# Attention on one NeuronCore: where TensorE's values product stands beside the transpose of the row maxima

## The reference

```
# "lat", layer 1: 16 heads of 16, rotary halves, causal
q, k, v = up(down(x))                  # latent projections
out = softmax(q k^T / 4 + causal mask) v
# "duo", layer 3: 16 heads of 16, two sets of keys, not causal
scores   = q k^T  / 4 ;  out_std = softmax(scores)   v
scores_p = q k'^T / 4 ;  out_p   = softmax(scores_p) v
out = (alpha * out_std + (1 - alpha) * out_p) W_O^T
```

## Time and profile before

| what | value |
|---|---|
| median of the runs | 3963.47 us (3 runs, 3954.07 to 3995.41) |
| span of the profiled execution | 3973.2 us |
| TensorE matmul busy | 3374.1 us, 85% of the span |
| VectorE busy | 2548.2 us, 64% |
| ScalarE busy | 2045.4 us, 51% |
| mean granted TensorE clock | 0.935 |
| lat units | about 545 to 843 us of the span |
| duo units | about 3190 to 3750 us of the span |

### The profile page before, as it was taken

How to read it: one execution, slowest core, us unless ns; L and a number is a source line. 1 busy time by engine, 2 the same in 40 slices (tenths; PEclk the granted TensorE clock), 3 DMA queues, 4 the chain that set the end, 5 groups by cost and what they waited for, 6 DMA issues and landing times. The chain is left out here.

```text
span 3973.2 us, 61781 instructions
## 1 busy us (share of the span) xinstructions
PE 3374.1 (85%) x20332; PEld 2517.7 (63%) x20332; DVE 2548.2 (64%) x3841; ACT 2045.4 (51%) x4432; POOL 1894.6 (48%) x1640
## 2 busy tenths in 40 slices
PE   1969989989986888888888888988887889999868
PEld 0659866668974666666666666666665655555544
DVE  6341155643126999999999999999997444444441
ACT  0332223332227777787777777877764344444422
POOL 0023200000316889888898889888885000000035
PEclk9879999999997999999999999999999989989965
DMA  3059710002951111111111111111110000000035
GB/s 97 2 185 334 268 63 1 1 18 106 331 207 34 44 33 44 33 44 36 42 45 44 37 42 34 43 42 35 33 43 22 26 1 1 1 1 1 3 109 174
DMA packets 133931, 264.41 MB, mean 67 GB/s; under 512 B 13888, under 2 KB 104504, under 8 KB 123096
## 3 DMA queue, kind: packets, MB, share of 16 engines
q1 hardware_dynamic: 122264, 229.24, 17.5%
q0 software_dynamic: 11328, 30.95, 2.3%
HBM read 233.64 MB, written 26.51 MB: 65 GB/s over the span
## 5 line engine op out<-in xcount | busy, mean ns | idle before, releaser
L1481 POOL TENSOR_TENSOR ssm_hc<-ssm_hs,ssm_cb 128x1024 f32<-128x1024 f32 x512 | 1204.5, 2356 | 179.0 <-PE ssm_py L1595 158.4
L1981 DVE TENSOR_TENSOR_SCAN ssm_hs<-ssm_da,ssm_pb 128x512 f32<-128x512 f32 x1024 | 1222.6, 1208 | 94.3 <-POOL ssm_hc L1481 89.5
L1595 PE MATMUL ssm_py<-ssm_hc,ident 128*128 128x256 f32 x4096 | 1068.6, 384 | 36.9 <-POOL ssm_hc L1481 36.9
L1794 ACT ACTIVATE ssm_da<-ssm_dt,ssm_an 128x255 f32<-128x255 f32 x2048 | 864.3, 498 | 192.9 <-DVE ssm_hs L1981 159.6
L1595 PEld LDWEIGHTS ssm_py<-ssm_hc,ident 128*128 128x128 f32 x4096 | 709.8, 192 | 116.9 <-POOL ssm_hc L1481 44.9
L1962 DVE TENSOR_TENSOR ssm_pb<-ssm_pb,ssm_dtu 128x512 f32<-128x512 f32 x832 | 564.0, 678 | 49.5 <-PE ssm_pb L1582 27.7
L1582 PE MATMUL ssm_pb<-ssm_bst,ssm_eyeb 96*128 96x256 bf16 x1664 | 328.6, 280 | 141.8 <-DVE ssm_hs L1981 125.9
L1582 PEld LDWEIGHTS ssm_pb<-ssm_bst,ssm_eyeb 96*128 96x128 bf16 x1664 | 133.3, 99 | 347.7 <-DVE ssm_hs L1981 249.4
L1134 DVE TENSOR_REDUCE duo_mxr<-duo_ring 128x4 f32<-128x1024 f32 x128 | 156.7, 1225 | 208.4 <-PE duo_ring L861 196.2
L2807 DVE TENSOR_TENSOR moe_hid<-moe_pu,moe_actg 128x512 f32<-128x512 f32 x71 | 49.1, 692 | 348.9 <-PE moe_pu L2450 348.9
L2450 PEld LDWEIGHTS moe_pu<-moe_xt,moe_up 128*128 128x128 f32 x2272 | 267.0, 193 | 6.4 <-ACT moe_xt L2570 3.0
(11 more groups left out here) (589 smaller groups left out, 5752.8 us busy)
## 6 DMA issues: line engine op xcount, KB each, us to landing
moe_up<-in_moe_up SPq DMA_DIRECT2D x72, 1024.0 KB, 7.4
ssm_cb<-ssm_c_dram SPq DMA_DIRECT2D x64, 1024.0 KB, 5.6
moe_down<-in_moe_down SPq DMA_DIRECT2D x72, 512.0 KB, 5.1
sw_wt<-in_sw_w SPq DMA_DIRECT2D x47, 192.5 KB, 2.7
moe_x_dram<-moe_tok SPq DMA_DIRECT2D x32, 128.0 KB
moe_yg<-moe_y_dram SPq DMA_DIRECT2D x16, 256.0 KB, 3.2
tok_w<-in_wd SPq DMA_DIRECT2D x4, 576.0 KB, 12.4
out<-h SPq DMA_DIRECT2D x1, 2056.0 KB, 7.3
```

The costliest lines, as they stand in the source:

```text
L1481: nc.gpsimd.tensor_tensor(hc[:, n % 2, part_], hs[:, n % 2, part_], cb[:, q % 2, part_, :], ALU.mult).then_inc(s["hc_done"], 1)
L1595: ins = nc.tensor.matmul(sums(j), k.ident[:], hc[:, n % 2, st, :], start=False, stop=(q == QN - 1 and st == NQ_ - 1 and j % 2 == 1))
L1794: ins = nc.scalar.activation(da[:, n % 2, 2 * m + o, 1:L], dt2[:, v, j, 1:L], ACT.Exp, scale=a_n[:, d, j, st:st + 1])
L1981: nc.vector.tensor_tensor_scan(two(hs[:, n % 2, 2 * m:2 * m + 2, :]), two(da[:, n % 2, 2 * m:2 * m + 2, :]), two(pb[:, p % 4]), 0.0, ALU.m ...
```

## The change

In `section_attention`, in TensorE's program alone, `values(u, A - 1)` is moved from behind `maxima(u + 1)` to ahead of it. Nothing is added and nothing taken away; the ring order is as before, since `values` takes no place in the ring.

```
                     if u >= G and g == 1:
                         last_spread(i - 1)
                         outward(i - 1)
+                    if 0 <= u < U:
+                        values(u, A - 1)
                     if 0 <= u + 1 < U:
                         maxima(u + 1)
-                    if 0 <= u < U:
-                        values(u, A - 1)
                     if A == 2 and 0 <= u + 1 < U:
                         last_key_rows(u + 1)
```

## The result

The changed kernel takes 4004.28 us (median of 8 runs, 3990.28 to 4024.75) where the kernel before takes 3964.28 us in the same comparison (8 runs). The ratio is 1.0092, with a 95% interval of 1.0063 to 1.0121: 0.9% slower, 25 to 48 us. I had said 3982, some 18 us slower, within 3957 to 4010. The sign held, and so did the mechanism; the size is twice what I had said. The time lies in the range, but beside the 4005 of rival C, the one with the clock, and not beside the forecast.

A forecast was written before the change was run, and what follows sets the result against it. TensorE was taken to bound the two attention layers; exposed `lower_query` waits, 16.7 us in lat and 1.8 in duo, add 18.5 to the 3963.5 us median, giving 3982 us within 3957 to 4010.

The forecast's parts named there:

- rival C: In duo or lat's g = 3, new idle time behind the maxima lowers the clock in more units: 4005 us, chance 0.22.
- the prices of the clock: Whole-kernel times if the clock changes: 3955 us if it keeps up, 4005 if it falls in more units.
- the sum: Unit-by-unit losses and gains of both layers: 16.7 us in lat plus 1.8 in duo, 18.5 us slower.
- What bounds, and which waits go: Both attention layers: TensorE sets the pace; its waits ahead of the maxima, 11.7 us in lat and 13.7 in duo, disappear.
- What comes instead: 1.12 and 1.54 us from the maxima to the scores: Behind the maxima, lat and duo: the bare chain through `lower_query` is exposed, 62 waits of some 0.7 us, 44 in all.
- lat's waits, 16.7 us: lat's units: losses of 0.76, 0.43, 0.51, 0.48 us for g = 0 to 3, 0.45 for each of the first two.
- duo's losses in g = 0, 1, 2: duo's units: scores come later by 0.54 us in g = 0 and 2, and 0.61 in g = 1.
- The rule on draining: Line 914 to 893 in duo: changing tiling mode drains TensorE, one more gap per unit, sum nearer its upper end.
- duo's g = 3, a gain of 1.3 us each: duo, g = 3: product done ahead at full clock brings scores 1.3 us earlier, seven times; at full clock throughout, 0.1 loss.
- Rival B: duo's g = 3: the product in the wait keeps the clock up, saving at most 36 us: 3955 us, chance 0.13.
- Rival D: Whole kernel: another wait later in the turn absorbs each shift, so nothing changes: 3964 us, chance 0.10.
- The signs that I had named: Profile after: waits moved behind line 886; lat about 2.2 us longer per image, duo nearly unchanged; half-clock stretches point to rivals.

The follow-up runs named there:

- e5: Kernel before with one more DVE operation (0.42 us, result unused) just ahead of `lower_query` in duo, old order: ratio 1.0001 (0.9974 to 1.0029).
- e6: Changed kernel with one more DVE operation (0.42 us, result unused) just ahead of `lower_query` in duo: ratio 1.0152 (1.0106 to 1.0198) against before.
- e3: Kernel before with the move only in duo and only where g = 3: ratio 0.9996 (0.9965 to 1.0026).
- e1: Kernel before with the move in lat alone, duo in the old order: ratio 1.0088 (1.0056 to 1.0120).
- e7: Kernel before, old order, with unused matmuls of 256 bf16 columns filling TensorE's waits in lat and duo: ratio 0.9869 (0.9828 to 0.9911).

## Why the prediction was right, and where it was off

The range held, but the forecast's own figure did not come out: 18.5 us against 36 to 40, short by some 10 us in lat and 8 in duo. What made the range wide enough were the prices of the clock, not the sum. In duo the sum's 1.8 us stand against 19 of waits, of which the clock gave back some 10.

*What bounds, and which waits go.* Right that TensorE bounds the layers; that ACT is busy for half of that or less doesn't hold in the first window quoted, where it is busy for 4.57 of 6.90 us. Of the 25.4 us ahead of the maxima 21.7 went. But 8.9 of them came back in lat ahead of the product itself. The sum had priced this as a later m.

*What comes instead: 1.12 and 1.54 us from the maxima to the scores.* Right: 1.16 and 1.56 were measured, and I had read them from the first units, which have no product to cover the chain. The added operation in e5 and e6 confirms that this is the cause. The wait itself, which I had put at 44 us, is 36.2.

*lat's waits, 16.7 us.* Right in kind, 3 us short: with the clock held 19.4. The terms that were short are g = 3 above all (0.78 for 0.48, seven times; 0.14 of it is the time between the exponential's end and the product's start), the first two units (0.71 for 0.45), and g = 1 (0.55 for 0.43); g = 2 was 0.1 too high.

*duo's losses in g = 0, 1, 2.* Each was mis-sized by 0.2 to 0.3 us. I had taken line 914 at lat's 0.79 us, "since the matmuls are the same sixteen". They are sixteen in both, but lat is causal, and half of them move 128 columns instead of 256. To line 886 it is 1.01 us in duo. The row of line 914 that I quoted as an upper bound, 1.07, was the better choice. The rule on draining that I had weighed (TensorEngine Tiling (Array Packing), Key Properties, in the Trainium skill) fits: the trace shows 0.41 us of idle ahead of line 886 in duo's weight loads where the column tiles end, and 0.20 in lat's. The whole 0.22 us lies there. It was in the bounds, not in the sum.

*duo's g = 3, a gain of 1.3 us each.* This is the step that failed. At full clock it is a loss of 0.49. The gain came wholly out of the half clock in one execution. I priced it against a row taken in a stretch at 0.50 (m + 4.82), though I wrote down myself that at full clock it would be a loss of 0.1. The half-clock stretches there come at different lengths in other executions of the same kernel. With the move in those units alone (e3) nothing was gained. The first two units of duo, where I had a gain of 0.77 each, gained 0.2 and 0.35 (14.52 to 14.30 us and 13.49 to 13.14).

*Rival C, the clock.* In lat it came true: I had named its g = 3 as the candidate, priced nothing for it, and left it out of the sum. It costs about 8 of lat's 27.5 us. In duo the opposite holds: the clock is granted a little more in the new order (0.94 to 0.95, against 0.90 to 0.94 in the four profiles of the old), which gives back half of the 20 us of waits there. So the two clocks nearly cancel: -10 us in duo (10 in place of 20.3) and +8 in lat (27.5 in place of 19.6). What is left is the loss by waits, 39 us.

*Rival B, that the product in the wait keeps the clock up.* In duo this is in part true, and not enough: about 55 us at half clock in place of 99 in the first pair of profiles, and in the mean of all some 10 us given back, where the rival had 36. *Rival D, that nothing changes,* is refuted by e1.

*The signs that I had named.* lat's four turns are longer by 2.5 us an image with the clock held, where I had said 2.2. duo's are nearly unchanged in the first pair, as I had said, but longer by 3.0 us with the clock held.

## What to carry to other kernels

Before moving work to fill a wait, ask what it covers now. Here the product stood between a request to another engine and the need for its answer, and covered that in nearly all 31 units of a layer, while the wait that it was moved into was there in one of four. A first or last unit that lacks the piece shows the bare cost, and did so to 0.04 us.

Price a gain at both clocks. A stretch at half clock in one profile may be there in one execution and not in the next, and a repeated stage needs more than one profile before a difference of a few us in it means anything.

If TensorE's lulls throw its clock down in a loop that it bounds, matmuls without use, placed where it waits anyway, can be worth more than a reordering: 1.3% here by the runs (0.9 to 1.7), of which the two layers' windows show 36 us, 0.9%.

## What the runs showed of the hardware

The granted clock fell in stretches where no single idle time of TensorE was above 1.5 us: in the old order of duo at each g = 3, with TensorE shown busy for 5.66 of the 6.90 us ahead. With some 1 us of that wait filled by nine matmuls of 256 columns, and lesser fillers elsewhere (e7), the granted clock of the layer is 0.99, and duo took 508 us in place of 530 to 548. I had not expected that a filler could save some 1% of a whole kernel, nor that the same instructions in the same order take 17 us more or less in one stage (530.4 and 547.7 us, at granted clocks of 0.94 and 0.90).
